# First chunk of the selective scan: statistics ahead of VectorE's diagonals, rstd by logarithm, gate projections and products in another order

## The reference

```python
x = x + 0.5 * _L0_ffn_ref(_layernorm(x), ...)   # 64 experts, top 3, capacity 64, hidden 512
x = x + _L0_attn_ref(_layernorm(x), ...)        # 256 channels, 16 states, 4 taps
x = x + 0.5 * _L0_ffn_ref(_layernorm(x), ...)

def _layernorm(x, axis=-1, eps=1e-05):
    m = jnp.mean(x, axis=axis, keepdims=True)
    v = jnp.var(x, axis=axis, keepdims=True)
    return (x - m) / jnp.sqrt(v + eps)

def _L0_attn_ref(x, W_in, conv_w, conv_b, W_x, W_dt, b_dt, A_log, D, W_out):
    proj = x @ W_in
    raw, gate = jnp.split(proj, 2, axis=-1)
    ...
    h = jax.nn.silu(conv + conv_b)
    ssm_p = h @ W_x
    ts, Bmat, C = jnp.split(ssm_p, [DTR, DTR + DST], axis=-1)
    dt = jax.nn.softplus(ts @ W_dt + b_dt)
    dA = jnp.exp(dt[..., None] * A)
    dBu = dt[..., None] * Bmat[:, :, None, :] * h[..., None]
    y = _ssm(dA, dBu, C)          # state = dA * state + dBu;  y = state . C
    y = y + h * D
    y = y * jax.nn.silu(gate)
    return y @ W_out
```

## Time and profile before

| | |
|---|---|
| median of 3 runs | 776.7 (774.32 to 778.22) |
| the profiled execution, its own time | 778.38 |
| its span, first to last instruction | 776.7 |
| mean granted TensorE clock | 0.927 of full speed |
| busy: TensorE, VectorE, ScalarE, GpSimd | 658.5, 602.5, 445.1, 478.5 |
| products of GpSimd, L1380 | 127 in 299.9 |
| scans of VectorE, L1301 | 128 in 285.9 |
| first scan, last scan start | 225.1, 573.5 |

### The profile page before, as it was taken

The page is one execution under the profiler, slowest core; times in us unless marked ns, Lnnn a source line. Parts: engine busy times, 40 slices in busy tenths (PEclk is TensorE's granted clock), DMA queues, the critical chain, the costliest instruction groups (busy, mean ns, idle before and its releaser), DMA issues.

```text
span 776.7 us, 27800 instructions
## 1 busy us (share of the span) xinstructions
PE 658.5 (85%) x11782; PEld 395.2 (51%) x11782; DVE 602.5 (78%) x1014; ACT 445.1 (57%) x925; POOL 478.5 (62%) x308
## 2 busy tenths in 40 slices
PE   6628999988857989899998989988989249999948
PEld 2514655557634445454544545454546135555647
DVE  7993555544799999999999999999898974555515
ACT  2401555553787889989898998787634103444420
POOL 3004666530149998989899898999961006666420
PEclk8858999998979999999999999999998659999979
DMA  8997999608364250524325151432009997998347
GB/s 271 399 332 229 365 377 315 223 29 320 83 145 105 60 139 6 138 57 116 81 70 129 29 134 38 116 83 57 3 3 347 359 269 238 373 378 269 131 149 300
DMA packets 87062, 141.07 MB, mean 182 GB/s; under 512 B 9444, under 2 KB 34670, under 8 KB 85665
## 3 DMA queue, kind: packets, MB, share of 16 engines
q1 hardware_dynamic: 82528, 126.99, 52.6%
q0 software_dynamic: 4416, 12.39, 4.3%
HBM read 112.02 MB, written 27.57 MB: 180 GB/s over the span
## 4 chain that ended last, share of the span: by engine, by line
PE 37%; POOL 28%; issue 18%; DVE 12%; DMA 3%; SPq 1%; ACT 1%; POOLq 0%; DVEq 0%; ACTq 0%
POOL BIG L1380 24%; PE ps L542 8%; PE ps L569 8%; PE ps L552 6%; PE ps L596 3%; PE ps L532 2%; POOL BIG L1395 2%; DVE BIG L1301 2%; PE ps L463 2%; POOL state_more L1387 2%; PE ps L510 2%; DVE stack L608 1%; PE ps L565 1%; PE ps L475 1%; DMA BIG<-y_dram 1%
## 5 line engine op out<-in xcount | busy, mean ns | idle before, releaser
L1380 POOL TENSOR_TENSOR BIG<-BIG,R 128x1024 f32<-128x1024 f32 x127 | 299.9, 2396 | 18.9 <-DVE BIG L1301 18.8
L1301 DVE TENSOR_TENSOR_SCAN BIG<-BIG,ps 128x1024 f32<-128x1024 f32 x128 | 285.9, 2271 | 5.5 <-PE ps L920 4.9
L920 PE MATMUL ps<-BIG,stack 64*32 64x128 f32 x8192 | 151.5, 278 | 34.5 <-DVE BIG L1301 33.0
L920 PEld LDWEIGHTS ps<-BIG,stack 64*32 64x32 f32 x8192 | 116.0, 107 | 112.1 <-DVE BIG L1301 81.6
L766 POOL DMA_INDIRECT R<-xn_dram,tok_idx x64 | 65.2, 1018 | 90.7 <-DVE row_idx L699 70.9
L777 POOL DMA_INDIRECT y_dram<-BIG,row_idx x64 | 64.6, 1010 | 64.0 <-DVE BIG L723 56.4
L708 DVE COPY BIG<-ps 128x512 f32<-128x512 f32 x64 | 44.3, 692 | 69.7 <-PE ps L542 69.7
L414 ACT ACTIVATE BIG<-BIG 128x512 f32<-128x512 f32 x64 | 40.4, 631 | 97.3 <-DVE BIG L715 95.7
L1168 ACT ACTIVATE BIG<-R,An 128x510 f32<-128x510 f32 x128 | 84.3, 710 | 5.6 <-DVE BIG L1301 5.5
L1168 ACT ACTIVATE BIG<-BIG,An 128x510 f32<-128x510 f32 x128 | 83.7, 708 | 0.2
L944 PE MATMUL ps<-BIG,fold 128*32 128x512 f32 x512 | 68.9, 612 | 1.3 <-POOL BIG L1380 1.3
(11 more groups left out here) (185 smaller groups left out, 965.8 us busy)
## 6 DMA issues: line engine op xcount, KB each, us to landing
BIG<-in_L_ffn_w SPq DMA_DIRECT2D x120, 512.0 KB
y_dram<-zeros SPq DMA_DIRECT2D x6, 2048.0 KB, 16.4
BIG<-y_dram SPq DMA_DIRECT2D x18, 512.0 KB, 9.1
BIG<-dt_dram SPq DMA_DIRECT2D x32, 256.0 KB, 4.7
R<-c_dram SPq DMA_DIRECT2D x32, 256.0 KB, 4.9
R<-dt_dram SPq DMA_DIRECT2D x32, 256.0 KB, 5.0
xn_dram<-R POOLq DMA_DIRECT2D x2, 2048.0 KB, 11.4
dt_dram<-state_more SPq DMA_DIRECT2D x16, 256.0 KB, 2.3
```

The lines of the kernel that those rows point to most:

```text
L920: last = nc.tensor.matmul(ps[CW * slot:CW * slot + CW, 2 * (st % 2) + b, :] .rearrange("p (g k s) -> p k g s", g=2, k=4)[:, k], dT[q % 2][ ...
L1301: nc.vector.tensor_tensor_scan(state[st % 3], dA[:, st % 6].rearrange("p b g t -> p (b g t)"), ps[:, u:u + 2, :].rearrange("p b n -> p (b ...
L1380: nc.gpsimd.tensor_tensor(prod[st % RP], state[st % 3].rearrange("p (b g t) -> p b g t", b=2, g=2), Cf[q % 2][:, 2 * gp:2 * gp + 2].rearra ...
```

## The change

All of it lies at the join.

- VectorE: after the memset come the 24 statistics and the first operation of rstd (variance + eps), then the two diagonals of chunk 0, then the rest of rstd.
- rstd of the 24 columns is made as exp(-0.5 * ln(v)) on ScalarE, two activations behind decay 1, and one Newton step on VectorE: 5 operations there instead of 13.
- VectorE: both halves of dt for chunk 1 stand behind the first scan.
- TensorE: the gate projections of chunk 0 move from step 1 to step 0, ahead of `dbu(3)`. ScalarE's gate copies move one step up, ahead of decay 5.
- GpSimd: in chunk 0 both halves of dt*u stand behind the first product, not ahead of the first and second.

```diff
+        def log_root_opened(S, i0, i1):
+            nc.vector.tensor_scalar(rs[:, 0, i0:i1], mv[:, i0:i1, 1], EPS, None, ALU.add).then_inc(S("rstd"), 1)
+
+        def log_root_scalar(e, S, i0, i1, n, m):
+
+            e.wait_ge(*S.at("rstd", n + 1))
+            nc.scalar.activation(rs[:, 2, i0:i1], rs[:, 0, i0:i1], ACT.Ln).then_inc(S("root"), 1)
+            e.wait_ge(*S.at("root", m + 1))
+            nc.scalar.activation(rs[:, 2, i0:i1], rs[:, 2, i0:i1], ACT.Exp, scale=-0.5).then_inc(S("root"), 1)
+
+        def log_root_closed(e, S, i0, i1, n, m):
 
             v, y, z, r = rs[:, 0, i0:i1], rs[:, 1, i0:i1], rs[:, 2, i0:i1], rstd[:, i0:i1]
+            e.wait_ge(*S.at("root", m + 2))
+            nc.vector.tensor_tensor(y, z, z, ALU.mult).then_inc(S("rstd"), 1)
...
@@ the first chunk's gates, TensorE @@
+                    if n == 0 and q == 0:
+                        gates(0, 0)
+                        gates(0, 1)
                     if n == 1:
                         if prev:
                             sum_states(q - 1, 1, 1, 1)
-                        if q == 0:
-                            gates(0, 0)
-                            gates(0, 1)
@@ ScalarE @@
             decays(0)
             decays(1)
+            log_root_scalar(e, MST, 8, NI, 12, 2)
             softplus_rest(1, 0)
...
-                    if q == 0 and n == 1:
+                    if q == 0 and n == 0:
                         gate_copy(0, 0)
                         gate_copy(0, 1)
@@ VectorE @@
+            stats(20, NI)
+            wait(e, "meanvar", NI)
+            log_root_opened(MST, 8, NI)
             diagonal(0, 0)
             diagonal(0, 1)
-            stats(20, NI)
-            statistics(8, NI, 12)
+            log_root_closed(e, MST, 8, NI, 12, 2)
...
-                    if q == 0 and n < C2:
-                        dt(1, n)
+                    if q == 0 and n == 0:
+                        dt(1, 0)
+                        dt(1, 1)
@@ GpSimd @@
-                    if n < C2 and q + 1 >= 0 and q + 1 < NQ:
+                    if n < C2 and q + 1 >= 0 and q + 1 < NQ and q != 0:
                         dtu(q + 1, n)
...
                         times_c(STEPS * q + n)
+                    if q == 0 and n == 0:
+                        dtu(1, 0)
+                        dtu(1, 1)
```

More of the change, by code:

```diff
@@ L93 @@
 STAT_TOTALS = dict(stats=NI, meanvar=NI, rstd=6, root=1)
-NEWTON = 13
 LN_TOTALS = dict(normed=24, normed_act=8, transposed=8, xT=8)
@@ L238, in macaron @@
         w2v = w2.rearrange("(a j) (p c) d -> j p a (c d)", a=2, c=HC)
[L241 to L247, removed]
-            v, y, z, r = rs[:, 0, i0:i1], rs[:, 1, i0:i1], rs[:, 2, i0:i1], rstd[:, i0:i1]
[L250 to L258, removed]
@@ new lines, in log_root_closed @@
+        def log_root_closed(e, S, i0, i1, n, m):
+            v, y, z, r = rs[:, 0, i0:i1], rs[:, 1, i0:i1], rs[:, 2, i0:i1], rstd[:, i0:i1]
+            e.wait_ge(*S.at("root", m + 2))
+            nc.vector.tensor_tensor(y, z, z, ALU.mult).then_inc(S("rstd"), 1)
+            e.wait_ge(*S.at("rstd", n + 2))
+            nc.vector.scalar_tensor_tensor(out=y, in0=y, scalar=-0.5, in1=v, op0=ALU.mult, op1=ALU.mult)\
+                .then_inc(S("rstd"), 1)
+            e.wait_ge(*S.at("rstd", n + 3))
+            nc.vector.scalar_tensor_tensor(out=r, in0=y, scalar=1.5, in1=z, op0=ALU.add, op1=ALU.mult)\
+                .then_inc(S("rstd"), 1)
+            e.wait_ge(*S.at("rstd", n + 4))
+            nc.vector.scalar_tensor_tensor(out=nmr[:, i0:i1], in0=mv[:, i0:i1, 0], scalar=-1.0, in1=r,
+                                           op0=ALU.mult, op1=ALU.mult).then_inc(S("rstd"), 1)
@@ L1070, in normalise @@
                 if q < 3:
-                    wait(e, "rstd", (6, 12, 12 + NEWTON)[q])
+                    wait(e, "rstd", (6, 12, 17)[q])
                 for j in range(4):
@@ L1254, in stats @@
                     nc.vector.bn_aggr(mv[:, i, :], st[:, i, :]).then_inc(M("meanvar"), 1)
-            def statistics(i0, i1, n):
-                wait(e, "meanvar", i1)
-                inverse_root(e, MST, i0, i1, n)
             for u in range(2):
```

## The result

| | before | changed |
|---|---|---|
| median of 22 runs each | 778.13 (774.32 to 781.20) | 774.62 (770.15 to 777.69) |
| the profiled execution, its span | 776.7 | 773.1 |
| mean granted TensorE clock | 0.927 | 0.937 |
| VectorE, L1268 / L1270 ahead of the first scan | 5.07 | 2.35 |
| from the join to the first scan | 11.08 | 7.88 |

The ratio is 0.9956, 95% interval 0.9941 to 0.9971: 3.5 us faster, between 2.3 and 4.6. The forecast gain was 4.7. It was counted from 776.7, the median of three runs; over 22 runs the kernel before takes 778.13. The "join" is the start of VectorE's small memset behind the last sum of the expert part. It lay at 214.0 in the profile before and at 216.1 in the one after, so times there are compared from the join on; first scan, sixth scan and so on are counted from 1.

A forecast was written before the change was run, and what follows sets the result against it. VectorE's own work between the expert part and the first scan was taken as the bound; 4.17 us saved to that scan plus 0.6 behind it gave -4.7, from 776.7 to 772.0, own range 770.3 to 773.8, overall 770.0 to 775.6.

The forecast's parts named there:

- same: Outcome class for the whole kernel: time within 0.5%, 3.9 us, of the kernel before; chance 0.35.
- faster: Outcome class for the whole kernel: a gain beyond 0.5%, 3.9 us; chance 0.60.
- Steps 1 and 2: VectorE at the join: statistics go first, then two diagonals find GpSimd idle, 2.35 instead of 5.07; saved 2.7 us.
- The first rival: At the join, GpSimd's diagonals hold up VectorE's statistics; first scan only 1.1 us earlier, 775.0 in all; chance 0.08.
- Step 3: rstd at the join: Ln and Exp on ScalarE 0.21 each, no table load; eight Newton operations gone, 1.7 us.
- Step 4: TensorE's first state input, formerly hidden, becomes the last wait; 1.5 of 1.7 reaches the first scan, 4.17 us earlier.
- step 6: TensorE behind the first scan: gate projections 1.7 at full clock, 2.82 at low; fourth scan at 228.7 or 229.9.
- Steps 5 to 8: Chunk 0 from first to sixth scan: reordered dt, gate projections and dt*u bring 0.6 us; scan 6 4.75 earlier.
- Whichever clock: Next chunk's first diagonal, behind the fourth scan, ends at 233.9 at either TensorE clock, since GpSimd's product 3 holds it.
- Step 9: From scan 6 to the end: old order, both VectorE's and GpSimd's chains shifted by the same 4.7 us, nothing lost.
- The third rival: TensorE's clock falls later in the chunk, 260 to 278 shifted; two low stretches cost 7.4 us, 779.4; chance 0.05.
- a granted clock of 0.5 after 245: Sign that the forecast is wrong: TensorE at its lower clock level later than 245 us in the profile.

The follow-up runs named there:

- keep_clock: The changed kernel with seven spare matmuls of 512 columns on TensorE where it otherwise waits, around chunk 1's dt projections and B transposes; 771.21 us in one run.
- pool_back: The changed kernel with GpSimd's two halves of dt*u put back ahead of the first and second product; 777.91 us in one run.
- psum_column: The changed kernel with VectorE's two diagonals of chunk 1 reading B's column from PSUM, TensorE's skip product waiting for both; 769.11 us in one run.
- psum_timed: The same edit to the changed kernel as psum_column, timed over 6 runs: 772.99 us, ratio 0.9927 to the kernel before.

## Why the prediction was right and where it was not

The measured 774.62 lies in the range of 770.0 to 775.6, but above 773.8, the end of the forecast's own. It is 2.6 above the 772.0. Of that, 1.4 is the base: the forecast started from 776.7, the median of three runs, where 22 runs give 778.13. The other 1.2 is gain that did not come. A gain of 0.44% is the case "same" (within 0.5%), to which I gave 0.35, and not "faster", to which I gave 0.60; the interval of 0.29% to 0.59% holds both. Direction and mechanism held; one term of the sum was too large.

- **Steps 1 and 2** held. The statistics kept their pace (0.2 each) beside GpSimd, whose diagonals took 3.76 as if alone, and VectorE's took 2.35, forecast 2.35. The first rival, exclusion by statistics, falls; the rule of the Trainium skill that I set against it ("SBUF — State Buffer", "SBUF: two separate sides") is now seen in both its parts: two SBUF inputs exclude GpSimd (2.98), one does not (1.19), nor do statistics.
- **Step 3** held: Ln 0.21, Exp 0.22, no table load, rstd 6.4 behind the join.
- **Step 4 is the one that failed.** It took "half of 2.02" for the first input, the upper clock of the earlier trace rows. Measured with the clock low, the first input ends 7.6 to 7.8 behind the join, not at 6.9. The first scan is 3.20 earlier and not 4.17; of the missing 0.97 the clock is 0.84 (7.88 against 7.04), and most of the rest the 0.16 between the input's end and the scan, which the sum left out. I had weighed the clock for the gate projections in step 6; but at the first input it is the very wait that ends last. What I wrote beside the "HAM oscillation" section of the Trainium skill ("TensorE: Matmul & The Clock Gate") was about the pause behind the second input: it would keep the high clock. Where the clock was up, in keep_clock, it did stay up through a pause of 1.62 there. In the changed kernel the clock had fallen before that, behind pauses of only 1.56 and 0.55, which the prediction did not consider. Held up artificially, the kernel gives what step 4 and the sum said: 7.04 (6.9 forecast), and 4.6 less at product 9 (4.75 forecast).
- **Steps 5 to 8** gave the right sum: first scan to scan 6 in 16.15, as forecast; the diagonal 2.98 where 1.7 to 2.9 was given; product 2 7.16 behind the first scan (7.15). The price in step 6 was misread, though: the clock rose within the 2.82 of the earlier trace rows. Wholly at the low level the projections take 3.78, at the upper one 1.98, not 2.82 and 1.7. "Whichever clock" is borne out by pool_back only as far as 3.02. For a clock that is low all through I estimate some 0.5 of delay at scan 5, since 1.96, 3.78 and 1.96 one after another put scan 4 past the end of GpSimd's product 3; no run shows it. The sum credits the saving of 0.6 to the removed wait of 1.27. Put back alone, dt*u's order costs 0.58 without that wait; the projections cost 1.17 or 0.2 by the clock.
- **Step 9** held as far as profiles can show it: from product 9 to the last scan before 320.03, after 319.54. But over the thirteen profiles this stretch lies between 317.95 and 321.40, and is 1.04 apart in two of one kernel (psum_column, psum_timed), so that a loss or gain of 1 us over the seven chunks would not be seen.
- **The third rival**, a low stretch late in the chunk, did not come: from 40 to 330 behind the join the clock stayed up. A low clock did decide, but earlier, at a smaller price. The sign "a granted clock of 0.5 after 245" was badly chosen: the changed kernel has one from 252.6 to 256.0 (36.5 behind the join), and the kernel before had the same from 254.3 to 257.7.

The rest between 3.8 at product 9 and the measured 3.5 is within the interval.

## What to carry to other kernels

When work that hid a TensorE step is removed, price that step at both clocks, not at the one it had while hidden, and check that the row you price it from lies wholly at one level. A VectorE operation with two SBUF inputs is cheap or dear by what GpSimd runs at that moment; move it to where GpSimd rests, or let one input come from PSUM, and then look at who waits for that PSUM bank. And attribute a gain by undoing edits singly and together: here the statistics' move alone gave 2.8, while the projections' move was worth 1.17 or 0.2 when undone alone, by the clock it met, and nothing more once dt*u's was undone too.

## What the runs showed of the hardware

- TensorE's granted clock fell to 0.50 when TensorE had worked 6.79 of the 8.90 us before, with pauses of 1.56 and 0.55. Seven spare matmuls in these pauses, 1.84 in sum, kept it at 1.00 in three of three profiles.
- The same program up to the first scan had the fall in some executions and not in others, and the first input started 5.75 behind the join in either case (5.88 in pool_back, where the clock fell already at 4.2). A single profile does not tell such a price.
- 64 small matmuls took 1.16 at the upper level and 1.96 at the lower, the gate projections 1.98 and 3.78.
- VectorE's BN_STATS ran 0.19 apart beside GpSimd's tensor_tensor, and neither was slower for it.
